# Ranks within a column summed by tile, three chunks a counting step, a placing pipeline over three steps, and the coefficients of the relations in the attention stage

## The reference, cut to what matters

```
x = x + mean over the incoming edges of (norm(x)[src] @ weight + bias)
x = x + experts(norm(x))       # graph attention (32,768 edges + self loops, 4 heads x 4 experts,
                               # softmax over each target's edges) gives scores; the best 2 of 4 experts
x = x + relu(segment_sum((norm(x) @ W[rel])[src] * edge_weight, dst))
        with W[r] = sum over b of w_comp[r, b] * bases[b]      # 32 relations, 8 bases
x = x + experts routed with a capacity (8 experts), layer norm
```

## Time and profile before

| | |
|---|---|
| median of 3 runs | 2321.53 us (2309.89, 2328.14, 2321.53) |
| the profiled execution | 2319.09 us, its span 2317.3 us |
| PE, PEld, DVE, ACT, POOL busy | 77%, 60%, 58%, 28%, 46% of the span |
| setup | 0 to 122.2 us |
| sum over neighbours | 122.2 to 810.6 us (688.4) |
| attention and experts | 810.6 to 1384.4 us (573.8) |
| sums by relation | 1384.4 to 1897.2 us (512.8) |
| third update | 1897.2 to 2317.3 us (420.1) |

### The profile page before, as it was taken

The page is one execution under the profiler, slowest core; times in us unless marked ns, Lnnn a source line. Parts: engine busy times, 40 slices in busy tenths (PEclk is TensorE's granted clock), DMA queues, the critical chain, the costliest instruction groups (busy, mean ns, idle before and its releaser), DMA issues. The chain is left out here.

```text
span 2317.3 us, 37611 instructions
## 1 busy us (share of the span) xinstructions
PE 1780.3 (77%) x9084; PEld 1395.4 (60%) x9085; DVE 1352.8 (58%) x3858; ACT 659.4 (28%) x1472; POOL 1057.5 (46%) x1102
## 2 busy tenths in 40 slices
PE   0667679999987778999997146667776739995996
PEld 0344456666655356777875136666666638883875
DVE  5488767777775663113134578888888851117325
ACT  1011025555554023223231143333433420003221
POOL 0616555555664104777775207777777730000000
PEclk9977668889998677999998568898889879997998
DMA  3302233333442022233234355555455554421001
GB/s 128 113 26 75 75 97 99 110 95 108 118 115 78 16 72 29 70 90 92 70 102 131 92 166 154 158 158 150 148 159 158 159 177 166 161 92 41 1 1 56
DMA packets 168773, 237.90 MB, mean 103 GB/s; under 512 B 36212, under 2 KB 125974, under 8 KB 165238
## 3 DMA queue, kind: packets, MB, share of 16 engines
q1 hardware_dynamic: 117984, 127.88, 17.5%
q0 software_dynamic: 47392, 105.58, 16.8%
q10 hardware_dynamic: 3318, 3.50, 0.5%
HBM read 180.73 MB, written 108.56 MB: 125 GB/s over the span
## 5 line engine op out<-in xcount | busy, mean ns | idle before, releaser
L451 POOL DMA_INDIRECT shared_space<-xn_table,edge_source x391 | 385.0, 985 | 372.6 <-PE part L735 214.5
L1886 PE MATMUL part<-coef,held 128*128 128x128 f32 x2368 | 344.3, 310 | 173.0 <-ACT held L1876 78.7
L451 POOL DMA_INDIRECT edge_rows<-xn_table,edge_source x391 | 373.9, 956 | 209.2 <-issue 112.1
L1886 PEld LDWEIGHTS part<-coef,held 128*128 128x128 f32 x2368 | 325.7, 222 | 191.7 <-DVE coef L1896 181.0
L735 PE MATMUL part<-shared_space,hot 128*128 x832 | 318.8, 518 | 95.1 <-DVE shared_space L1056 45.7
L1908 DVE SCALAR_TENSOR_TENSOR window_sums<-window_sums,fine_keep,part 128x256 f32 x592 | 284.3, 480 | 68.0 <-PE part L1886 51.7
L735 PEld LDWEIGHTS part<-shared_space,hot 128*128 128x128 f32 x832 | 177.8, 244 | 179.0 <-issue 162.1
L1876 ACT ACTIVATE held<-edge_rows 128x256 f32 x592 | 197.2, 404 | 307.7 <-POOLq L448 171.7
L1350 POOL DMA_INDIRECT gall<-attention_table,attention_source x256 | 245.7, 960 | 78.0 <-issue 77.7
L1056 DVE TENSOR_TENSOR shared_space<-shared_space,part 128x257 f32 x416 | 175.1, 421 | 136.0 <-PE part L735 90.3
L1896 DVE SCALAR_TENSOR_TENSOR coef<-iota,fine_target,slot_coefs 128x128 f32<-128x128 f32 x592 | 205.2, 348 | 0.6 <-DMA slot_coefs<-coefficients 0.6
(11 more groups left out here) (441 smaller groups left out, 2285.9 us busy)
## 6 DMA issues: line engine op xcount, KB each, us to landing
basis_sums<-window_sums SPq DMA_DIRECT2D x75, 1024.0 KB
z<-basis_sums SPq DMA_DIRECT2D x25, 1024.0 KB, 4.9
expert_rows<-ys SPq DMA_DIRECT2D x20, 640.0 KB, 3.5
shared_space<-expert_rows SPq DMA_DIRECT2D x25, 512.0 KB, 5.2
W<-in_L_ffn_W SPq DMA_DIRECT2D x24, 512.0 KB, 5.0
low_rows<-attention_digits SPq DMA_DIRECT2D x32, 256.0 KB
xn_table<-shared_space SPq DMA_DIRECT2D x10, 640.0 KB, 3.8
shared_space<-xn_table,edge_source POOLq DMA_INDIRECT x391
```

The lines of the kernel that those rows point to most:

```text
L451: pool.indirect_dma_start(rows[:, b % ring, 0:D], None, table, bass.IndirectOffsetOnAxis(ap=esrc[:, b:b + 1].bitcast(U32), axis=0)).then_i ...
L1886: mm = nc.tensor.matmul(part[:, n, c * P:(c + 1) * P], held[n][:, c * P:(c + 1) * P], coef[n][:, :, :].rearrange("p b w -> p (b w)"), star ...
```

## The change

- Counting has `PER_STEP` = 3 chunks a step, so it takes 11 steps, and two indicators are made ahead. Basing starts with step 12, placing with step 17, and `AFTER` is 49. There are four banks for the sums.
- Basing spreads the scans over three quarters (2, 2 and 1), ACT makes the bf16 copies, DVE's subtractions come in the fourth quarter.
- Only the low digits are stored and broadcast. `equals` compares them alone (bias -1), and the rank is summed by tile: `same` is multiplied with the chunk's tile indicator instead of ones, and DVE's product with the same indicator picks the right one. Both halves of a comparison go through one bank.
- Placing is a pipeline: in step b PE does `places_of(b-1)`, the first half of `equals(b)`, `permute(b-2)`, the second half. DVE does the row indicator of b+1, the place of b-1, the tiles of b and the carry of b-1. ACT has a half of `same` of b, a half of the columns of b-1, and again. SP's load of chunk b still waits for `placed` of chunk b-2, which PE now does in step b-1. The place is split with float arithmetic, and the carry compares with a bf16 `iotab`.
- `segments` has one pass a quarter, the rest follows the additions of step 50. The last step of PE waits for the end of it (`PASSED`).
- The coefficients leave the sum over neighbours. Their 37 rounds stand in the attention stage between L1701 and the wait at L1704, with a bf16 indicator and bf16 transposes, one `relt_ps`, one `relhot_t` and one `coef_ps`. `coefs` stays in SBUF until `sum_relations` (it is lent before to the sort and to `W2`); store and load go. On ACT the copies stand between two Exp. `wcomp` is loaded in the attention stage.
- Other buffers of the attention stage are lent (`hid[1]`, `W1[0]`).

```diff
-        STEPS, SET, BANKS = KA // STEP, 2, 2
+        STEPS, SET, BANKS = KA // STEP, 2, 4
         SETS = STEP // SET
         LAG = NT
-        CHUNKS_S, PER_STEP = GT // SORT, 4
-        COUNTED, BASED = CHUNKS_S // PER_STEP, CHUNKS_S // PER_STEP + 1
+        CHUNKS_S, PER_STEP = GT // SORT, 3
+        PAIRS = CHUNKS_S // (2 * PER_STEP)
+        COUNTED = -(-CHUNKS_S // PER_STEP)
+        BASED = COUNTED + 1
         PLACED = BASED + NT // CT
         AFTER = PLACED + CHUNKS_S
-        COEFS_AT = (0, PLACED, PLACED + 10, RS)
-        assert PLACED % 2 == 0 and PLACED + 2 < RS < AFTER < STEPS and RS % 2 == 1 and RS - PLACED - 10 <= PLACED
+        assert CHUNKS_S == PAIRS * 2 * PER_STEP + 2 and COUNTED == 2 * PAIRS + 1 and AFTER + 3 == STEPS
...
-            sp.wait_ge(cleared, 1)
-            for q in range(QT):
-                sp.dma_start(wcomp[q * RELS:(q + 1) * RELS, q, :], a["L1_gnn_w_comp"]).then_inc(wc_in, 16)
...
-                    sp.wait_ge(placed, b + 1)
-                for rows_b, k in ((low_rows, 0), (tile_rows, 1)):
-                    sp.dma_start(rows_b[:, b % 2, :], digits_dram[k, b * SORT:(b + 1) * SORT, :].rearrange("t e -> (t e)")
-                                 .partition_broadcast(rows_b.shape[0])).then_inc(digits_in[b % 2], 16)
-                for lo, hi in zip(COEFS_AT, COEFS_AT[1:]):
-                    if b == hi - PLACED + 1:
-                        sp.wait_ge(coefs_made, hi + 1)
-                        sp.dma_start(coefs_dram[:, lo * RQ:hi * RQ, :], coefs[:, 0:(hi - lo) * RQ, :]).then_inc(coefs_out, 16)
-            sp.wait_ge(coefs_out, 16 * 3)
+                    sp.wait_ge(placed, b - 1)
+                sp.dma_start(low_rows[:, b % 2, :], digits_dram[b * SORT:(b + 1) * SORT, :].rearrange("t e -> (t e)")
+                             .partition_broadcast(P)).then_inc(digits_in[b % 2], 16)
...
+            def same_half(b, q, first=False):
+                if not first:
+                    act.wait_ge(placed, b)
+                act.wait_ge(equal_ready, b * 2 + q + 1)
+                nc.scalar.activation(same[:, q * 4:(q + 1) * 4, :].rearrange("p t e -> p (t e)"), equal_ps[:, :],
+                                     ACT.Relu, bias=minus1[:, :]).then_inc(same_ready, 1)
+
+            def columns_half(b, k, q, first=False):
+
+                act.wait_ge(place_ready, b + 1)
+                if not first:
+                    act.wait_ge(permuted, b)
+                act.wait_ge(cols_ready, b * 2 + q)
+                for t in range(4):
+                    nc.scalar.activation(apart[:, t, :], edges.slot_iota[:, 0:GT], ACT.Abs,
+                                         bias=col[k][:, q * 4 + t:q * 4 + t + 1]).then_inc(apart_ready, 1)
+                act.wait_ge(apart_ready, b * 8 + q * 4 + 4)
+                nc.scalar.activation(cols[:, q * 4:(q + 1) * 4, :], apart[:, :, :], ACT.Relu,
+                                     bias=one[:, :], scale=-1.0).then_inc(cols_ready, 1)
+
+            def placing(b, k, first=False):
+                same_half(b, 0)
+                columns_half(b - 1, 1 - k, 0, first=first)
+                same_half(b, 1)
+                columns_half(b - 1, 1 - k, 1, first=first)
...
+                for r in range(CT):
+                    act.wait_ge(prefixed, w * CT + r + 1)
+                    nc.scalar.activation(one_of(base[0], w, r), upto[:, r, :], ACT.Copy).then_inc(halved, 1)
...
+            def equals(b, k, q, first=False):
+
+                if q == 0:
+                    pe.wait_ge(hots_ready, b + 1)
+                if not first:
+                    pe.wait_ge(same_ready, b * 2 + q)
+                nc.tensor.matmul(equal_ps[:, :].rearrange("p (t e) -> p t e", e=P), identb[:, :],
+                                 earlier[:, :].unsqueeze(1).to_broadcast([P, 4, P]), start=True, stop=False)
+                for t in range(4):
+                    low = low_hot[k][:, q * 4 + t, :]
+                    mm = nc.tensor.matmul(equal_ps[:, t * P:(t + 1) * P], low, low, start=False, stop=(t == 3))
+                mm.then_inc(equal_ready, 1)
...
-                    mm = nc.tensor.matmul(to, same[:, t, :], onesb[:, :], start=False, stop=True)
+                    mm = nc.tensor.matmul(to, same[:, t, :], tiles[k][:, t, :], start=False, stop=True)
...
+            def placing(b, k, fill=0):
+
+                if fill != 1:
+                    places_of(b - 1, 1 - k)
+                yield
+                equals(b, k, 0, first=(fill == 1))
+                yield
+                if not fill:
+                    permute(b - 2)
+                yield
+                equals(b, k, 1)
...
+            step(AFTER, ending())
+            step(AFTER + 1)
+            permute(CHUNKS_S - 1)
             nc.tensor.matmul(sorted_ps, zeros[:, 0:P], zeros[:, :], start=False, stop=True).then_inc(sort_replies, 1)
...
+                    V.tensor_tensor_scan(upto[:, r, :], one_of(count, w, r), one_of(count, w, r), gstart[:, ds(w * CT + r, 1)],
+                                         ALU.add, ALU.max).then_inc(prefixed, 1)
+                    if r % 2 or r == CT - 1:
+                        yield
                 for r in range(CT):
-                    link.note(V.tensor_copy(one_of(base[0], r), upto[:, r, :]))
-                yield link.wait()
-                for r in range(CT):
-                    link.note(V.tensor_tensor(one_of(base[1], r), upto[:, r, :], one_of(base[0], r), ALU.subtract))
-                yield link.wait()
+                    dve.wait_ge(halved, w * CT + r + 1)
+                    link.note(V.tensor_tensor(one_of(base[1], w, r), upto[:, r, :], one_of(base[0], w, r), ALU.subtract))
+                link.wait()
...
+            def place_of(b, k):
+
+                dve.wait_ge(placed, b + 1)
+                link(V.tensor_tensor(own, place_ps, tiles[k], ALU.mult))
+                link(V.tensor_reduce(ahead[:, :], own, AX.X, ALU.add))
+                link(V.tensor_scalar(place[:, :], ahead[:, :], 0.5 - GT / 2, 1.0 / GT, ALU.add, ALU.mult))
+                link(V.tensor_scalar(place[:, :], place[:, :], WHOLE, None, ALU.add))
+                link(V.tensor_scalar(row[k][:, :], place[:, :], WHOLE, None, ALU.subtract))
+                link(V.scalar_tensor_tensor(col[k][:, :], row[k][:, :], float(GT), ahead[:, :], ALU.mult, ALU.subtract))
+                dve.sem_inc(place_ready, 1)
+
+            def carry(b, k):
+                for t in range(SORT):
+                    V.tensor_scalar(carried[:, t, :], iotab[:, :], row[k][:, t:t + 1], value[:, ds(b * SORT + t, 1)],
+                                    ALU.is_equal, ALU.mult).then_inc(carried_ready, 1)
+
+            def placing(b, k, ii, fill=0, last=False):
+
                 if not last:
                     hots(b + 1, 1 - k, ii + k)
                 yield
-                link.note(V.tensor_tensor(tiles[k], other[:, ds(b * SORT, SORT)].unsqueeze(2).to_broadcast([P, SORT, NT]),
-                                          iota[:, 0:NT].unsqueeze(1).to_broadcast([P, SORT, NT]), ALU.is_equal))
+                if fill != 1:
+                    place_of(b - 1, 1 - k)
                 yield
-                dve.wait_ge(placed, b + 3)
-                link.wait()
-                link(V.tensor_tensor(own, place_ps, tiles[k], ALU.mult))
-                link(V.tensor_reduce(ahead[:, :], own, AX.X, ALU.add))
-                link(V.tensor_copy(place[:, :], ahead[:, :]))
-                link.note(V.tensor_scalar(place_i[:, 0, :], place[:, :], 8, None, ALU.arith_shift_right))
-                link(V.tensor_scalar(place_i[:, 1, :], place[:, :], GT - 1, None, ALU.bitwise_and))
-                link.note(V.tensor_copy(row[k][:, :], place_i[:, 0, :]))
-                link(V.tensor_scalar(col[k][:, :], place_i[:, 1, :], -1.0, None, ALU.mult))
-                dve.sem_inc(place_ready, 1)
+                tiles_of(b, k).then_inc(tiles_ready, 1)
                 yield
-                dve.wait_ge(permuted, b + 2)
-                for t in range(SORT):
-                    V.tensor_scalar(carried[:, t, :], iota[:, :], row[k][:, t:t + 1], value[:, ds(b * SORT + t, 1)],
-                                    ALU.is_equal, ALU.mult).then_inc(carried_ready, 1)
+                if fill != 1:
+                    if fill != 2:
+                        dve.wait_ge(permuted, b - 1)
+                    carry(b - 1, 1 - k)
...
+            step(AFTER, parts=last_places())
+            segments_made = segments()
+            step(AFTER + 1, parts=segments_made)
+            for _ in segments_made:
+                pass
+            step(AFTER + 2, more=False)
...
+                act.wait_ge(relt_ready, i + 1)
+                nc.scalar.activation(relhot_t[:, :, :].rearrange("p q e -> p (q e)"), relt_ps, ACT.Copy).then_inc(relt_copied, 1)
...
+            def turn_relations(i):
+                pe.wait_ge(relhot_ready, i + 1)
+                for q in range(RQ // QT):
```

(29 more changed lines are left out.)

385 lines of the change are left out of this document (164 added, 221 removed).

## The result

The kernel after takes 2343.7 us (median of 5 runs, 2340.21 to 2347.66), the kernel before 2321.53 in the runs beside it: a ratio of 1.0097, 95% interval 1.0072 to 1.0123. It is slower by about 1%. The profiled execution spans 2344.6 us against 2317.3, so 27.3 us have to be found. I had forecast 7 less.

A forecast was written before the change was run, and what follows sets the result against it. No engine was taken as full; a circle of handoffs through the row load was to set placing. Terms -2 - 17.5 - 34.5 - 18 + 66 - 1 = -7 against 2319.09 gave 2312 us, own range 2296 to 2342, 8-in-10 range 2262 to 2358.

The forecast's parts named there:

- Coefficients in the attention stage: Attention stage: 37 rounds of 2.6 us, none overlapping, 98 us with 31.6 covered by the gathers' hole: +66 us.
- the coefficient rounds are long: Rival, attention stage: rounds of 3.2 us, +22, and a late PE register load in placing, +10: 2344 us; chance 0.08.
- Rest: Setup and relation stage: coefficients' load worth nothing, small loads, a DVE operation and a store: -1 us.
- The attention stage up to the carry copy: Attention stage before the coefficient rounds: three small DVE copies sit before the weights land, 0 us.
- Placing: Neighbour stage, placing steps: a circle through the row load of 12.7 us, above DVE's 10.3; 399 against 433.3: -34.5 us.
- The late load: Rival, placing: row landing above 3.2 us is paid 29 times; at 5.0 us +52, 2364 us; chance 0.14.
- The circle does not pass through the banks: Placing: argument against the rival that only DVE binds, whose support was the four PSUM banks; no size of its own.
- nothing binds in placing but DVE: Rival, placing: rows land before DVE asks, 32 steps at 10.3 give 330, 69 less: 2243 us; chance 0.13.
- Basing: Neighbour stage, basing steps: copies to ACT, less relation work, 8 us of waiting gone; 54.4 against 71.9: -17.5 us.
- Counting and totals: Neighbour stage: ten counting steps 99 us, two totals steps 23, together 122 against 123.9: -2 us.
- closing: End of the neighbour stage: three steps instead of six, 41 against 59.3: -18 us.
- the carry in bf16: Placing: no gain counted; by the skill's estimate 0.03 us an operation, 9 us in the stage at most.

The follow-up runs named there:

- coef2: Kernel after with the coefficient rounds two deep (two PSUM banks each, two indicators, two copies): 1.0024, 1.0034 and 1.0052 of the kernel before.
- all3: Kernel after with four row buffers, coefficient rounds two deep, clearing write cut in 16: 0.9894, 0.9906, 0.9893 of the kernel before; single execution (all3_look) 2251.70 us beside 2320.25.
- zsplit: Kernel after with DVE's clearing write of the relation stage's window sums cut in 16: 1.0096 and 1.0124 of the kernel before.
- banks2: Kernel after with two PSUM banks for the neighbour sums in place of four: 2407.12 us in one execution, beside 2319.38 for the kernel before.
- rows4: Kernel after with four low-digit row buffers, not two: 1.0023, 1.003, 1.0034 of the kernel before; single execution (rows4_look) 2294.89 us beside 2320.25.

## Why the prediction was wrong

The bottom line failed: I forecast 2312 us, 7 less and "within 1%", and measured are 2343.7, 22 more by the medians, with an interval (1.0072 to 1.0123) that lies wholly above 1. 2343.7 lies in the range of 2262 to 2358 and 1.7 us above the forecast's own 2296 to 2342. The misses of the table add up to 34 us, by the steps of the prediction:

- **Coefficients in the attention stage: +66, measured +81.9.** This is the step that failed most, 16 us: the term "eight matmuls (41.8 us / 37 = 1.13)". The mechanism was right: 37 rounds in a row, no wait left for the gathers, DVE's part beside it. The size of a round was off, 3.03 us for 2.6. I took PE's matmuls at the mean of a stage with a granted clock of 0.80, and the stretch runs at 0.50, where they start 0.21 us apart. From the first of the eight to the end of the four transposes it is 2.34 us (1241.68 to 1244.02) for my 1.75, and the rest of the round is 0.69 for my 0.89. The transposes kept their size, 0.61 for 0.62. The trace of the kernel before had shown the hole at 0.50. coef2 and all3 split the round: 2.08 us is PE alone, 0.95 are ACT's copy and the handoffs. The rival "the coefficient rounds are long" had the size, 3.2 us a round, with a chance of 0.08. That its 2344 us in sum meets the measured time is luck: 10 of it were a late register load of PE in placing, and the misses below are others.
- **Rest: "the load of the coefficients ... is worth nothing, since gathers start there at the same time".** The load was worth nothing, but the gathers behind the first start 8 us late, and the stages behind the combination took 8.5 us more. zsplit and all3 show that it takes the whole clearing write (a first gather of 0.94 for 8.98 us). The prediction looked only at what DVE waits for, and not at what POOL's first gather meets. Why the kernel before escapes it, with the write at the same distance, isn't shown.
- **The attention stage up to the carry copy: 0, measured +9.2.** I had named only three DVE copies there. From the last addition to the carry copy it is 457.0 us before and 465.0 after, but 458.5 in the kernel before's second trace, 464.2 in banks2, and 458.9 and 457.9 in rows4_look and all3_look, which have the same three copies. So the copies explain at most 2 us. Some of the rest is at the start of the experts, where PE waits for DVE: 1.59 us before, and the 12 matmuls behind it take 2.86 us at a granted clock of 1.00; 3.92 us after, and they take 5.49 at 0.50. The kernel before's second trace waits 3.65 us there and is granted 0.80 and 0.86 in the windows 916 to 921 and 921 to 926, so a part of this varies from one execution to the next. What else there is stays open. Two windows of the kernel after, and behind them the kernel before at the same place:

```profile
855.00:860.00 5.00, 2.17 (x11) 1.55 (x9) 4.33 (x12) 0.00 (x0) 3.78 (x5) 0.97 0.25 67
860.00:865.00 5.00, 3.91 (x9) 3.19 (x10) 1.36 (x6) 0.00 (x0) 3.78 (x5) 0.50 0.12 8
```

```profile
926.00:931.00 5.00, 3.59 (x17) 3.18 (x18) 1.93 (x8) 0.00 (x0) 3.77 (x4) 1.00 0.10 8
```

- **Placing: -34.5, measured -29.9.** The circle is there link by link, and 29 steps from 318.9 to 691.4 us make 12.84 each, for 12.7. The load is 3.6 us where I took 3.2, from the row of 2.7. The late load was a rival from 4.2 us on; it didn't get there. "The circle does not pass through the banks" holds with four banks only: with two it does, by 42 us (banks2). What lies below was a circle of PE and ACT at 11.5 us (rows4), which the prediction has nowhere, and not DVE's 10.3: the rival "nothing binds in placing but DVE" was dead with or without the load. DVE's own pace was lower than 10.3, if anything: 12.84 less the 3.26 that it waits for the load leaves 9.6 (an estimate), and the wait is longer than the 2 us that I gave as a sign.
- **Basing: -17.5, measured -12.7.** Of the 8 us that I gave to the stored coefficients and the banks, banks2 shows 1.6 for the banks. Four steps are 11.3 us for 10.9. The last takes 14.0 us: PE waits 5.08 us for the end of basing before it turns to placing, and DVE then 3.25 us for its sums.
- **Counting and totals: -2, measured -4.4; closing: -18, measured -22.7; setup -1, -2.2.** Ten counting steps took 99.2 us for 99. The rest is two totals steps of 20.3 for 23, and closing at 36.6 for 41.

Two sums in the prediction are slightly off: the terms of DVE's pace make 10.2, not 10.3, and those of the closing's second step 17, not 17.5. Neither changes what follows from them.

On the carry in bf16 (2.14 us for eight): it takes 1.88 after, 0.03 us less an operation. That is the size that the Trainium skill (VectorE: DVE Perf Modes, The perf-mode tier table) gives by the estimate in the prediction. It shortens nothing here, since DVE waits 3.26 us for the load in the same step.

On the first gather: the Trainium skill (SBUF — State Buffer, Who interferes with whom) has a DVE instruction in a two-port mode and POOL exclude each other: whoever issues first keeps the shared ports for the whole instruction, and the other fully blocks. It does not list a clearing write among the instructions that do so on this chip. The trace agrees in that a whole gather, 0.95 us, lies behind the end of the write. It does not agree in the order, since the gather is the one that starts first, by 1.14 us. Nor does the kernel before agree: its gathers from 1385.72 on take 0.95 us each inside the same write. So the rule alone would not have told which of the two kernels pays.

## What to carry to other kernels

Price an operation that moves to another place at the clock of the place it moves to, and not at its old stage's mean. The row of the hole had 0.50 before the change. Before work goes into a hole, compare its length with the hole: here 114 us went into 32 and cost 82, and two-deep buffers gave back 35 of them at once.

Where a pipeline is shortened, follow each buffer from its release to its next use, also those that one compute engine frees for another (ACT's columns wait for PE's `permute`). Here two more buffers took the load out of the circle, and the next circle was close: 12.8 us, then 11.5, with DVE's own pace at an estimated 9.6.

A kernel's stages meet at their starts: what the first gather, load or clear of a stage runs into is worth a line of its own in a forecast.

## What the runs showed of the hardware

PE, busy for all 40 us with the matmuls and transposes of the coefficient rounds (coef2_again), was granted 0.50 all the time. The expert stage of the kernel before, busy for all 69 us from 931 on, has 1.00. What tells the two apart no run shows.

In the kernel after a POOL gather of 0.94 us takes 8.98 when DVE clears 128x8192 in one write of 6.88 that begins 1.14 us behind its start. It takes 0.94 when the same area is cleared in 16 writes of some 0.5. In the kernel before, with one write at the same distance, it takes 0.94 too.
